# Row maxima of an attention stage as tensor_scalar passes that carry a running minimum

## What is computed

```
attn = einsum('bhqd,bhkd->bhqk', q, k)        # b = 1, q = k = 2048
attn = softmax(attn, axis=-1)
attn = round(attn / s) * s,  s = max(attn) / 255   # per query row
out  = einsum('bhqk,bhkd->bhqd', attn, v)
```

## Time and profile before

| | us |
|---|---|
| median of 3 runs | 2473.56 (2473.38 to 2480.1) |
| the profiled execution's own time | 2477.05 |
| its span, first to last instruction | 2475.3 |
| VectorE busy, whole span | 1785.8 (72%) |
| TensorE busy | 1950.7 (79%) |
| ScalarE busy | 1634.9 (66%) |

### The profile page before, as it was taken

The page is one execution under the profiler, slowest core; times in us unless marked ns, Lnnn a source line. Parts: engine busy times, 40 slices in busy tenths (PEclk is TensorE's granted clock), DMA queues, the critical chain, the costliest instruction groups (busy, mean ns, idle before and its releaser), DMA issues. The chain is left out here.

```text
span 2475.3 us, 42289 instructions
## 1 busy us (share of the span) xinstructions
PE 1950.7 (79%) x12019; PEld 1265.1 (51%) x12084; DVE 1785.8 (72%) x2918; ACT 1634.9 (66%) x2564; POOL 501.7 (20%) x410
## 2 busy tenths in 40 slices
PE   5886999999999999995466776767767677773698
PEld 4664878777787877773353222222222222223587
DVE  4996676777767687775646888888888888885333
ACT  3775888888888888881436767677676767772111
POOL 0000555555555555550000000000000000001000
PEclk9997999999999999997876555555555555556799
DMA  1002000000000000001004878778777877881000
GB/s 57 17 8 86 0 26 0 25 0 25 25 0 25 0 25 0 25 0 49 7 0 77 153 146 149 147 148 149 146 148 147 149 148 147 149 155 52 18 17 17
DMA packets 558402, 164.84 MB, mean 67 GB/s; under 512 B 535073, under 2 KB 550817, under 8 KB 558369
## 3 DMA queue, kind: packets, MB, share of 16 engines
q1 hardware_dynamic: 558368, 164.44, 33.4%
HBM read 28.09 MB, written 2.10 MB: 12 GB/s over the span
## 5 line engine op out<-in xcount | busy, mean ns | idle before, releaser
L1222 ACT ACTIVATE levels<-s_ps,nb,qstep 128x1024 int16<-128x1024 f32 x512 | 612.2, 1199 | 267.6 <-DVE nb L1180 267.6
L1170 DVE TENSOR_REDUCE mx<-s_ps 128x1 f32<-128x512 f32 (+1 forms) x768 | 659.5, 865 | 98.3 <-PE s_ps L1115 81.5
L1115 PE MATMUL s_ps<-kT,qT 48*128 48x512 bf16 x1024 | 521.9, 612 | 264.5 <-ACT levels L1222 262.6
L588 DVE SCALAR_TENSOR_TENSOR xs<-x_ps,cw,xs 128x508 f32<-128x508 f32 (+2 forms) x393 | 291.3, 741 | 174.8 <-ACT xs L510 137.4
L1115 PEld LDWEIGHTS s_ps<-kT,qT 48*128 (+1 forms) x1024 | 82.4, 104 | 514.3 <-issue 490.9
L479 PE MATMUL o_ps<-wo,hid 128*128 x1024 | 243.0, 380 | 4.7 <-DVE acc L575 4.7
L644 POOL TENSOR_TENSOR hid<-y,sg 128x512 f32<-128x512 f32 x128 | 175.4, 1370 | 278.6 <-ACT sg L532 185.8
L1125 PEld LDWEIGHTS ao_ps<-vi,levels_T 128*128 128x128 f16 x4096 | 129.5, 105 | 185.2 <-issue 185.2
L1340 POOL TENSOR_TENSOR o_rstd<-o_mv,o_minus_half 128x16 f32<-128x16 f32 x1 | 2.9, 2902 | 1037.7 <-DVE o_mv L902 1037.7
L479 PEld LDWEIGHTS o_ps<-wo,hid 128*128 128x128 f32 x1024 | 192.6, 189 | 40.2 <-issue 9.8
L510 ACT ACTIVATE xs<-x_ps,cb,cw 128x512 f32<-128x512 f32 x131 | 101.9, 778 | 116.9 <-PE x_ps L431 116.9
(11 more groups left out here) (195 smaller groups left out, 3356.3 us busy)
## 6 DMA issues: line engine op xcount, KB each, us to landing
w_raw<-winT_dram SPq DMA_DIRECT2D x18, 512.0 KB, 4.5
wo_raw<-woutT_dram SPq DMA_DIRECT2D x9, 512.0 KB, 5.6
levels_T<-levels SPq DMA_TRANSPOSE x256, 4.3
w_bc<-winT_dram SPq DMA_DIRECT2D x18, 128.0 KB, 2.2
xT<-xT_dram SPq DMA_DIRECT2D x4, 512.0 KB, 7.9
acc<-x_dram SPq DMA_DIRECT2D x1, 2048.0 KB, 11.0
ctxT<-ctxT_dram SPq DMA_DIRECT2D x4, 512.0 KB, 7.5
out_dram<-f_out SPq DMA_DIRECT2D x16, 128.0 KB, 1.7
```

What stands on the lines that cost most here:

```text
L588: dve.scalar_tensor_tensor(to, x_ps[:, :, 0:SEQ - s], cw[:, head, TAPS - 1 - s], to, ALU.mult, ALU.add).then_inc(chain if s < TAPS - 1 els ...
L1115: return pe.matmul(s_ps[:, BANKS[h % 2][chunk], :], qT[:, bass.ds(round_, 1), h % NH, :].rearrange("p b t -> p (b t)"), kT[:, h % NH, at:a ...
L1170: dve.tensor_reduce(mx[:, h % 2, at:at + 1], src, AX.XY if what == "cd" else AX.X, ALU.max).then_inc(max_chain, 1)
L1222: act.activation(levels[:, s, half * HALF:(half + 1) * HALF].rearrange("p (c k) -> p c k", c=2), s_ps[:, first:first + 2, :], ACT.Exp, bia ...
```

## The change

The maxima become `tensor_scalar` passes with an accumulator output. Each multiplies the scores by `nstep` (negative), so that the minimum is wanted, and accumulates the minimum; its start value is 3e38 for "b" and the result of the pass before it for "cd" and "a". The products themselves go to `spill`, in bf16, which nobody reads. Behind "a" stands -step * maximum already, and one addition of ln 255 makes `nb`. `mall` goes. Each pass and the addition waits, held, for the one ahead of it. `nstep` holds one query tile and is made anew for each (`steps`), ahead of "b" of its first head. `sums` keeps two tiles instead of 16. TensorE no longer waits for `nstep` before its first score.

```diff
-        mx = sb("mx", [P, 2, 3])
-        mall = sb("mall", [P, 2])
+        low = sb("low", [P, 2, 3])
         nb = sb("nb", [P, 2])
-        nstep = sb("nstep", [P, BATCH, NH])
+        spill = sb("spill", [P, HALF], BF16)
+        nstep = sb("nstep", [P, NH])
...
-        sums = sb("sums", [P, BATCH, NH, 2])
+        sums = sb("sums", [P, 2, NH, 2])
...
-            pe.wait_ge(consts, 1)
...
-            def maxima(n, h, what):
...
-                dve.wait_ge(ready, n + 1)
-                dve.tensor_reduce(mx[:, h % 2, at:at + 1], src, AX.XY if what == "cd" else AX.X,
-                                  ALU.max).then_inc(max_chain, 1)
-
-            def bias(n, qt, h):
-
-                u = h % 2
-                dve.wait_ge(max_chain, n * 4 + 3)
-                dve.scalar_tensor_tensor(mall[:, u:u + 1], mx[:, u, 0:1], mx[:, u, 1:2], mx[:, u, 2:3],
-                                         ALU.max, ALU.max).then_inc(max_chain, 1)
-                dve.wait_ge(max_chain, n * 4 + 4)
-                dve.tensor_scalar(nb[:, u:u + 1], mall[:, u:u + 1], nstep[:, bass.ds(qt, 1), h % NH], LN255,
-                                  ALU.mult, ALU.add).then_inc(nb_ready, 1)
+            def lowest(n, h, what):
+
+                u = h % 2
+                bank = BANKS[u]
+                ready, first, banks, init, to = {
+                    "b": (b_ready, bank["b"], 1, 3.0e38, low[:, u, 0:1]),
+                    "cd": (cd_ready, bank["c"], 2, low[:, u, 0:1], low[:, u, 1:2]),
+                    "a": (a_ready, bank["a"], 1, low[:, u, 1:2], low[:, u, 2:3])}[what]
+                dve.wait_ge(ready, n + 1)
+                if what != "b":
+                    dve.sem_inc(held, 1)
+                    dve.wait_ge(low_chain, n * 3 + (1 if what == "cd" else 2))
+                elif not (isinstance(n, int) and n == 0):
+                    dve.sem_inc(held, 1)
+                    dve.wait_ge(nb_ready, n)
+                dve.sem_inc(held, 1)
+                dve.tensor_scalar(spill[:, 0:banks * GT], s_ps[:, first:first + banks, :].rearrange("p c k -> p (c k)"),
+                                  nstep[:, h % NH:h % NH + 1], init, ALU.mult, ALU.min,
+                                  accum_out=to).then_inc(low_chain, 1)
+                if what == "a":
+                    dve.wait_ge(low_chain, n * 3 + 3)
+                    dve.sem_inc(held, 1)
+                    dve.tensor_scalar(nb[:, u:u + 1], to, LN255, None, ALU.add).then_inc(nb_ready, 1)
+
+            def steps(at):
+
+                if not (isinstance(at, int) and at == 0):
+                    dve.wait_ge(nb_ready, at * NH)
+                    dve.sem_inc(held, 1)
+                dve.tensor_scalar(nstep[:, :], qstep[:, bass.ds(at, 1), :].rearrange("p q h -> p (q h)"),
+                                  -1.0, None, ALU.mult).then_inc(step_chain, 1)
+                dve.wait_ge(step_chain, at + 1)
+                dve.sem_inc(held, 1)
...
             def body(qt):
                 for h in range(NH):
                     n = qt * NH + h
+                    if h == NH - 1 and exists(qt, h, 1):
+                        steps(qt + 1)
                     if exists(qt, h, 1):
-                        maxima(n + 1, h + 1, "b")
+                        lowest(n + 1, h + 1, "b")
                     if h == LAG and exists(qt, 0, -1):
                         finish(qt, qt - 1)
                     if exists(qt, h, 1):
-                        maxima(n + 1, h + 1, "cd")
-                        maxima(n + 1, h + 1, "a")
-                        bias(n + 1, qt if h < NH - 1 else qt + 1, h + 1)
+                        lowest(n + 1, h + 1, "cd")
+                        lowest(n + 1, h + 1, "a")
```

More of the change, by code:

```diff
@@ L1076, in attention @@
         o_ps = ctx.enter_context(nc.psum_tensor("ao_ps", [P, GT], F32))
-        consts, a_ready, b_ready, cd_ready, max_chain, nb_ready, ab_exp, cd_exp, pv_done, scaled, chain = (
-            sem("at_" + n) for n in ("consts", "a_ready", "b_ready", "cd_ready", "max_chain", "nb_ready", "ab_exp",
+        step_chain, a_ready, b_ready, cd_ready, low_chain, nb_ready, ab_exp, cd_exp, pv_done, scaled, chain = (
+            sem("at_" + n) for n in ("step_chain", "a_ready", "b_ready", "cd_ready", "low_chain", "nb_ready", "ab_exp",
                                      "cd_exp", "pv_done", "scaled", "chain"))
@@ L1183, in finish @@
+            def steps(at):
[6 more added lines that the diff above has]
+                dve.sem_inc(held, 1)
             def finish(qt, last):
-                both = sums[:, bass.ds(last, 1), :, :].rearrange("p q h s -> p (q h) s")
+                both = sums[:, bass.ds(last % 2, 1), :, :].rearrange("p q h s -> p (q h) s")
@@ L1202, in body @@
                     if exists(qt, h, 1):
-                        maxima(n + 1, h + 1, "cd")
-                        maxima(n + 1, h + 1, "a")
-                        bias(n + 1, qt if h < NH - 1 else qt + 1, h + 1)
[L1207 to L1212, removed]
+                        lowest(n + 1, h + 1, "cd")
+                        lowest(n + 1, h + 1, "a")
+            steps(0)
+            lowest(0, 0, "b")
+            lowest(0, 0, "cd")
+            lowest(0, 0, "a")
             rounds(dve, body)
@@ L1223, in exps @@
                                ACT.Exp, bias=nb[:, u:u + 1], scale=qstep[:, bass.ds(qt, 1), h],
-                               accum_out=sums[:, bass.ds(qt, 1), h, half:half + 1].rearrange("p q s -> p (q s)")
+                               accum_out=sums[:, bass.ds(qt % 2, 1), h, half:half + 1].rearrange("p q s -> p (q s)")
                                ).then_inc(cd_exp if half else ab_exp, 1)
```

## The result

The changed kernel takes 2567.56 us (median of 4 runs, 2564.3 to 2569.3), the kernel before 2474.32 beside it: a ratio of 1.037, 95% interval 1.0351 to 1.0389. Forecast was 2565. The profiled execution has a span of 2562.5 us, 87.2 more than before. All of it lies in the attention stage: from the first exponential to the last it is 899.2 us before (1328.8 to 2228.0) and 987.6 after (1327.5 to 2315.1).

The account below looks back on a forecast made before the run. A ring of waits among VectorE, ScalarE and TensorE (3.49 us a head) bounds attention now, VectorE's 3.79 afterwards; 67 + 15.5 + 4.5 + 4.5 = 91.5 us on the median of 2473.56 gives 2565 us, range 2480 to 2630.

Parts of the forecast that it names:

- VectorE becomes the bound: Attention stage: VectorE's own row, 3.79 us a head with no hole, sets the turn after the change.
- Operands, 0.05 and 0.12: Per-partition operands in VectorE's passes: one adds about 0.05 us, two about 0.12; b 0.74, cd 1.34, a 0.81.
- R1: Rival, attention: operands free and accumulator reads at -0.04 us each, ring shorter and VectorE keeping up; 2433 us, chance 0.09.
- R3: Rival, VectorE's passes: one price vanishes, operands free (2491 us) or reads at -0.04 us (2497 us); chance 0.18.
- The accumulator read, 0.05: Writing out VectorE's accumulator, three times a head: 0.154 us long, starting 0.10 before the pass's end, adding 0.05 each.
- R4: Rival, VectorE's passes: accumulator read waits for the pass to end, +0.10 us each, turn 4.10; 2645 us, chance 0.11.
- Held gaps, 4 x 0.147: VectorE, ahead of cd, a, `nb` and b: each held wait leaves 0.147 us, 0.59 us a head.
- Steps, finish and loop's edge: VectorE's per-round work: steps 4.5 us in all, finish between b and cd 4.5 us more; no change priced for the edge.
- The sum: Attention stage: 67 us in the loop, 15.5 in written-out heads, 4.5 for steps, 4.5 for finish; 91.5 us more.
- The ring at 3.48, with 0.3 to spare: Cycle of waits among ScalarE, TensorE and VectorE: 3.48 us a head, score "a" ready 0.3 before VectorE reaches it.
- R2, free waits: Rival, VectorE: held waits cost nothing, each pass starting on the end of the one in front; 2420 us, chance 0.03.

Follow-up runs that it names:

- e2: Changed kernel with constant -1 instead of the step in the three passes and the step multiplied in `nb`: 2541.81 us, ratio 1.0246.
- e3: Changed kernel with the same waits, each fused with the instruction behind it instead of held: 2460.62 us, ratio 0.9924.
- e10: Changed kernel with only the held wait between pass a and `nb` fused: 2533.13 us, ratio 1.0221.
- e6: Changed kernel with each pass's two waits swapped, VectorE's own first and the one for the scores last: 2651.74 us, ratio 1.0711.
- e1: Kernel before, keeping its `tensor_reduce` maxima, with the changed kernel's order of held waits added: 2608.60 us, ratio 1.0521.

## Why the prediction was right, point by point

- **VectorE becomes the bound.** Right: its wait for scores left the list of waits, and e2, e3, e10 and e6 all move the time by what they take from or add to its row.
- **Operands, 0.05 and 0.12.** Right: 751 and 810 ns for 512 columns, 1344 for 1024, against 0.74, 0.81 and 1.34 forecast. The price came from three pairs of other instructions and carried over. One of the pairs was no clean one: the `scalar_tensor_tensor` with 742 ns reads a second tensor besides the operand, so that its agreement is luck. e2 gives the clean price, 692 ns without and 751 with one. R1 and the first half of R3 fall with it.
- **The accumulator read, 0.05.** Too high. It lasts 83 ns and starts 0.07 to 0.08 ahead of the pass's end (1706.57 + 0.751 = 1707.32; the read runs from 1707.24 to 1707.32), so about 0.01 is added. By ScalarE's analogy and VectorE's smallest operation it would have been 0.154 long. That is -0.12 us a head. 83 ns lies between the 154 taken and the 59 of R3's second half, whose price of -0.04 isn't borne out either. The overlap of 0.10 that the step was built on was read in the heads written out; inside the loop b and cd of the kernel before take 1.94 in a row, 0.03 more than their sum. R4 falls. As the Trainium skill says ("VectorE: DVE Perf Modes", section "Two Vector instructions with no wait between them"), the read is an instruction of its own; the trace has 768 of them, three a head.
- **Held gaps, 4 x 0.147.** Too low: 0.167, 0.167, 0.155, 0.187, together 0.68 against 0.59, +0.09 a head. Behind `nb` stand two waits and a step of 0.15 us only to cover the first; in e2, where `nb` lasts 0.21, the gap is 0.16.
- Both together make 3.755 for 3.79: 224 x 0.26 = 58 us for 67. In the written-out heads the turn is 3.72 (pass b starts at 1331.37 and 1335.09): 31 x 0.43 = 13 for 15.5. That a turn was 0.20 shorter in these heads before was put down to `mall` to `nb` alone. That is 0.10 of it; the rest lies between the end of `nb` and the exponential, 0.04 instead of 0.15. It changes nothing in the sum.
- **Steps, finish and loop's edge.** Under-priced: from `nb` to b across the steps 0.87 instead of 0.19, so 0.68 a round for a forecast of 0.30; the finish 1.75 from b to cd instead of 0.92, 0.83 for 0.74; the edge 0.67 for 0.19, 0.48 where it was put at no change. Together 1.99 us a round above 16 turns. Before it was 0.9 (13 rounds take 738.8 us, 56.83 each, less 16 x 3.495). The difference of 1.08 makes 15 us in 14 rounds where 9 was put down.
- The sum: 58 + 13 + 15 = 86, measured 88.4 in the stage. The forecast's 91.5 was this near by luck, with errors on both sides: reads too dear, gaps and rounds too cheap. What bounds the stage, and why, was no luck.
- **The ring at 3.48, with 0.3 to spare.** Wrong in size without harm: with 0.11 for a held wait I had left out that two follow on one another. e1 shows 0.33 from the arrival of score "a" (0.58 behind its start) to a, and e2 a ring of 3.65. In the changed kernel only about 0.13 was to spare, since score "a" is there 0.46 ahead of the pass and 0.33 of that is needed.
- **R2, free waits.** Refuted by e1, e3, e6 and e10.

## What to carry to other kernels

Before work is moved off a chain of waits onto an engine, sum that engine's whole row per turn, gaps included: here VectorE had 0.35 us to spare, and the change put 0.68 us of gaps on it. Let a wait go with its instruction where that is free of races. Where waits must be held, put the one that comes last at the end, and count each one behind it. Where waits are fused, count a second one too, most of all ahead of an instruction that an engine further on waits for.

## What the runs showed of the hardware

- A held wait (the wait on a semaphore instruction of its own) leaves 0.147 to 0.187 us on VectorE between the end of one instruction and the start of the next, 0.22 where an address comes from a register (e1, `mall` to `nb`). A fused one leaves 0.03 to 0.06 in most places inside the loop, 0.12 from `nb` to b (e3), and 0.13 from `mall` to `nb` in the kernel before, where the address comes from a register (0.03 where it doesn't).
- A held pair whose condition is long met still costs 0.11 to 0.16 us if it stands behind the wait that comes last (e6: 84 us in all), and about 0.01 ahead of it (0.167 against 0.155).
- Two fused waits ahead of a pass leave 0.12 to 0.13 us in the heads written out (e3), where one leaves 0.04. Where scores come last, a pass with two fused waits starts 0.08 to 0.11 us later behind them than an instruction with one does (0.71 to 0.73 against 0.62, and 1.15 to 1.18 against 1.07).
- VectorE's accumulator read takes 83 ns and ends about 0.01 us behind its pass. A per-partition operand adds 0.06 us to a pass: 692, 751 and 810 ns with none, one and two for 512 columns, 1284 and 1344 with one and two for 1024 (e2 and the changed kernel).
